# Value products in float16 halves, a score bound of 53, a branch marked ahead and the second norm by blocks, in a transformer layer

## The reference

```
q, k, v = lora(x, Wq..), lora(x, Wk..), lora(x, Wv..)     # x @ W.T + 2 * x @ B.T @ A.T
s = q k / 4 + slope[h] * (i - j);  s = -1e30 where j > i
a = softmax(s) v @ Wp.T
x1 = layernorm(x + a)
gates, experts = top-2 of softmax(x1 @ Wg), normed; rows over the capacity are dropped
y = sum over the two of gate * (gelu(x1 @ W1[e] + b1[e]) @ W2[e] + b2[e])
out = layernorm(x1 + y)
```

## Time and profile before

| | us |
|---|---|
| median of 3 runs (lowest, highest) | 1194.21 (1194.05, 1194.89) |
| the profiled execution | 1195.21 |
| its span, first to last instruction | 1193.2 |
| busy in it: TensorE, ScalarE, VectorE | 1124.1, 867.6, 629.0 |
| exponentials, first start to last end | 29.0 to 760.5 |

### The profile page before, as it was taken

One profiled execution on the slowest core, in us unless ns is written; L12 is line 12 of the kernel. 1 busy time (PEld: TensorE's weight loads), 2 busy tenths in 40 slices (PEclk: granted clock), 3 DMA queues, 4 the chain that ended last, 5 costly groups with the idle time before them and its releaser, 6 DMA issues. The chain is left out here.

```text
span 1193.2 us, 23954 instructions
## 1 busy us (share of the span) xinstructions
PE 1124.1 (94%) x8592; PEld 503.7 (42%) x8592; DVE 629.0 (53%) x1832; ACT 867.6 (73%) x1109; POOL 300.4 (25%) x377
## 2 busy tenths in 40 slices
PE   9999999999999999999999979879999999999980
PEld 4333232222323222222222111267777777777760
DVE  5744342232366435734352401558777777777757
ACT  2889999999999999999999999434334433433315
POOL 5521111111123222230323120022333333333340
PEclk9999999999999999999999999979999999999995
DMA  6843341422321331122321100263553652552217
GB/s 180 186 108 82 91 95 51 94 68 88 93 75 57 113 71 60 53 89 68 83 70 43 44 19 17 91 183 49 119 114 48 134 118 32 124 133 27 25 19 282
DMA packets 119301, 104.20 MB, mean 87 GB/s; under 512 B 59223, under 2 KB 104508, under 8 KB 119184
## 3 DMA queue, kind: packets, MB, share of 16 engines
q1 hardware_dynamic: 101720, 76.90, 24.8%
q0 software_dynamic: 15968, 24.12, 9.3%
q10 hardware_dynamic: 1496, 1.68, 0.5%
HBM read 48.07 MB, written 47.96 MB: 80 GB/s over the span
## 5 line engine op out<-in xcount | busy, mean ns | idle before, releaser
L1502 ACT ACTIVATE prob<-ps_s 128x1024 f32<-128x1024 f32 (+4 forms) x841 | 703.8, 981 | 28.9 <-PE ps_s L1382 27.0
L1401 PE MATMUL ps_o<-prob,v_aug 128*17 128x512 f32 (+3 forms) x3236 | 404.0, 567 | 8.8 <-ACT prob L1502 5.8
L2469 ACT ACTIVATE hid<-ps_h,b 128x384 f32<-128x384 f32 (+1 forms) x192 | 107.3, 560 | 229.1 <-PE ps_h L2412 223.5
L1382 PE MATMUL ps_s<-qop,kop 51*128 51x512 f16 (+3 forms) x1618 | 252.4, 368 | 10.8 <-ACT prob L1502 4.4
L1382 PEld LDWEIGHTS ps_s<-qop,kop 51*128 51x128 f16 x1618 | 61.7, 93 | 334.1 <-ACT prob L1502 307.1
L2428 PE MATMUL ps_y<-w2s,hs 128*128 128x256 bf16 (+1 forms) x1728 | 189.8, 273 | 0.1
L1586 DVE COPY acc<-ps_o 32x512 f32<-32x512 f32 (+2 forms) x108 | 74.2, 687 | 218.8 <-PE ps_o L1401 216.4
L2412 PE MATMUL ps_h<-xs,w1s 128*128 128x384 bf16 (+1 forms) x1152 | 186.4, 315 | 0.0
L2386 POOL DMA_INDIRECT result<-y,entry x72 | 116.5, 1618 | 249.0 <-DVE y L2500 218.3
L2428 PEld LDWEIGHTS ps_y<-w2s,hs 128*128 128x128 bf16 (+1 forms) x1728 | 160.0, 99 | 25.4 <-issue 3.1
L1538 POOL TENSOR_SCALAR_AFFINE_SELECT prob<-prob 128x256 f32<-128x256 f32 (+1 forms) x179 | 69.3, 400 | 300.1 <-ACT prob L1502 298.2
(11 more groups left out here) (201 smaller groups left out, 688.0 us busy)
## 6 DMA issues: line engine op xcount, KB each, us to landing
w<-in_W SPq DMA_DIRECT2D x16, 1024.0 KB, 7.9
slots_x<-empty POOLq DMA_DIRECT2D x12, 520.0 KB, 3.9
qop<-fparts_q SPq DMA_DIRECT2D x42, 128.0 KB, 4.8
aT<-attnT SPq DMA_DIRECT2D x16, 256.0 KB
x_all<-in_x SPq DMA_DIRECT2D x8, 512.0 KB
result<-x_all SPq DMA_DIRECT2D x8, 512.0 KB, 3.5
x_all<-result SPq DMA_DIRECT2D x8, 512.0 KB, 7.2
out<-x_all SPq DMA_DIRECT2D x8, 512.0 KB, 2.6
```

The source lines that it names most:

```text
L1382: mm = pe.matmul(ps_s[:, u.p % SLOTS_S, e, a.q0:], o.key(e, a.h, a.kt), o.query(e, a.h, a.b, a.q0), start=True, stop=True)
L1401: mm = pe.matmul(ps_o[32 * c:32 * c + VW, a.q0:], o.v[:, a.kt, a.h], prob[:, t % RING, c % 2, c // 2, a.q0:], start=a.first, stop=a.last)
L1502: act.activation(prob[:, t % RING, n, e:z, q0:], ps_s[:, u.p % SLOTS_S, e:z, q0:], ACT.Exp, scale=1.0 / (SCALE * SCALE)).then_inc(exp_done, 1)
L2469: act.activation(hid[:, q % HB, 0:w], ps_h[:, q % HB, 0:w], ACT.Gelu_apprx_tanh, bias=b1[:, e, q % HC:q % HC + 1]).then_inc(gelu, 1)
```

## The change

The bound falls from 55 to 53, and with it the tiles of four heads; the plan of turns and all tables are new. Values of blocks 2 to 7 are made from the float16 halves of x and of the value weights, which are split once (dve_split_values, at SPLIT_V_AT; their largest value joins the test). The general path, which used values made in float32, now makes them itself. Because value tiles read the halves of x, these can be overwritten later only; the splits move to 2 and 1 turns ahead of the first half tile and the reductions to 1 and 3 turns after it. The flag is loaded 4 turns ahead of the branch, the place is marked as the hint of the branch, and the branch is written with br_ne. The second norm goes by single blocks; ScalarE takes the root (function Sqrt, warmed by one instruction right behind the experts), VectorE its reciprocal and one Newton step.

```diff
-BOUND = 55.0
+BOUND = 53.0
...
 LATER = [int(c) for c in
-            ('6664664226425344534642334246422334264245645445534246424444444246424435345364534453453444444642424344'
...
+            ('4664564234534454534642434246423445353133444455342345323453423345323344233555555645453534446645556456'
-HALF_AT = {2: (17, 19, 21, 23, 25, 27, 29, 31), 3: (45, 47, 51, 55, 57, 59, 63, 67), 4: (87, 89, 95, 97, 100, 103, 106, 111), 5: (135, 139, 141, 148, 151, 154, 160, 164), 6: (193, 200, 205, 208, 212, 216, 225, 229), 7: (264, 266, 271, 277, 285, 294, 296, 298)}
+HALF_AT = {2: (17, 19, 21, 23, 25, 27, 29, 31), 3: (45, 47, 50, 54, 56, 58, 61, 66), 4: (87, 89, 94, 96, 98, 100, 102, 109), 5: (133, 136, 138, 146, 148, 152, 157, 161), 6: (191, 198, 203, 206, 210, 213, 222, 224), 7: (260, 263, 269, 273, 281, 291, 293, 295)}
-NORM_AT = {0: 4, 1: 15, 2: 33, 3: 69, 4: 114, 5: 168, 6: 236, 7: 305}
+NORM_AT = {0: 4, 1: 14, 2: 33, 3: 68, 4: 113, 5: 166, 6: 232, 7: 302}
-VALUE_AT = {0: (0, 2), 1: (6, 9, 11, 13), 2: (35, 37, 39, 41), 3: (71, 73, 81, 84), 4: (118, 121, 128, 132), 5: (175, 177, 180, 188), 6: (239, 243, 250, 261), 7: (309, 324, 326, 335)}
+VALUE_AT = {0: (0, 2), 1: (6, 8, 10, 12), 2: (35, 37, 39, 41), 3: (70, 73, 80, 84), 4: (116, 120, 126, 130), 5: (173, 175, 178, 186), 6: (236, 240, 247, 256), 7: (306, 319, 324, 330)}
-SETUP_TURN, BOUND_TURN = 76, 338
+SETUP_TURN, BOUND_TURN = 75, 334
...
+SPLIT_V_AT = {5: 0, 7: 1, 9: 2, 11: 3}
...
         if _p[2:] == (0, 0):
             for _k in range(4):
-                SPLIT_X_AT[_t - 5 + _k] = (_p[1], _k)
+                SPLIT_X_AT[_t + (-2, -1, 1, 3)[_k]] = (_p[1], _k)
+            assert _p[1] == 2 or VALUE_AT[_p[1] - 1][-1] < _t - 2
...
+ANNOUNCED = 4
...
+@contextmanager
+def only_if(nc, eng, name, announced):
+
+    flag, at = announced
+    eng.br_ne(flag, 0, on_true=name + "_taken", on_false=name + "_past").branch_hint(at)
+    with nc.body(name + "_taken", valid_engines=bass.OrderedEngineSet([eng.engine])):
+        yield
+        eng.br(name + "_past")
+    nc.switch_bb(name + "_past")
...
     def pe_value(j, pe, n, s, out):
-        pe.wait_ge(j.x_loaded[n % 2], 16 * (n // 2 + 1))
-        for c in range(2):
-            mm = pe.matmul(out, j.xT[:, n % 2, c, s * P:(s + 1) * P], j.weff[:, 2, c, :], start=(c == 0), stop=(c == 1))
+        cols = slice(s * P, (s + 1) * P)
+        if n < 2:
+            pe.wait_ge(j.x_loaded[n], 16)
+            for c in range(2):
+                mm = pe.matmul(out, j.xT[:, n, c, cols], j.weff[:, 2, c, :], start=(c == 0), stop=(c == 1))
+        else:
+            pe.wait_ge(j.wv_done, 3)
+            pe.wait_ge(j.xs_done, n - 1)
+            for i, (a, b) in enumerate(FPARTS):
+                for c in range(2):
+                    mm = pe.matmul(out, j.xs[:, a, c, cols], j.wv_low[c] if b else j.wv_high[:, c],
+                                   start=(i == 0 and c == 0), stop=(i == len(FPARTS) - 1 and c == 1))
         mm.then_inc(j.v_mm, 1)
...
+    def dve_split_values(j, dve, k):
+
+        w = j.weff[:, 2]
+        if k == 0:
+            dve.wait_ge(j.weff_done, 6)
+            dve.wait_ge(j.w_loaded, 16 * 2)
+            dve.tensor_scalar(j.wv_high, w, SCALE, None, ALU.mult).then_inc(j.wv_done, 1)
+        elif k == 1:
+            dve.wait_ge(j.wv_done, 1)
+            for c in range(2):
+                dve.scalar_tensor_tensor(out=j.wv_low[c], in0=w[:, c], scalar=SCALE, in1=j.wv_high[:, c], op0=ALU.mult,
+                                         op1=ALU.subtract).then_inc(j.wv_done, 1)
+        else:
+            dve.tensor_reduce(j.peak[:, k - 2, NB - 1:], j.wv_high.rearrange("p c d -> p (c d)"), AX.X,
                               (ALU.max, ALU.min)[k - 2]).then_inc(j.peaks, 1)
...
     def dve_split_x(j, dve, n, k):
...
             if n > 2:
-                dve.wait_ge(j.proj_mm, j.done(n - 1, 3))
+                dve.wait_ge(j.v_mm, n * KT)
...
     def dve_value(j, dve, n, s, bank):
         dve.wait_ge(j.v_mm, n * KT + s + 1)
-        dve.tensor_copy(j.o.v[:, n * KT + s, :, 0:DH], bank[:, 0:D].rearrange("p (h d) -> p h d", h=H)).then_inc(j.v_out, 1)
-        dve.tensor_copy(j.r.xg[:, n * KT + s], bank[:, D:D + E]).then_inc(j.v_out, 1)
+        scale = 1.0 if n < 2 else 1.0 / SCALE
+        dve.tensor_scalar(j.o.v[:, n * KT + s, :, 0:DH], bank[:, 0:D].rearrange("p (h d) -> p h d", h=H), scale, None,
+                          ALU.mult).then_inc(j.v_out, 1)
+        dve.tensor_scalar(j.r.xg[:, n * KT + s], bank[:, D:D + E], scale, None, ALU.mult).then_inc(j.v_out, 1)
...
     def flag_of(j, eng):
         eng.wait_ge(j.bnd_step, 11)
-        return eng.value_load(j.flag[0:1, 0:1], min_val=0, max_val=1)
+        flag = eng.value_load(j.flag[0:1, 0:1], min_val=0, max_val=1)
+        return flag, eng.mark_branch_hint_location()
...
+                    if t == FLAG_TURN - ANNOUNCED:
+                        announced = j.flag_of(pe)
                     if t == FLAG_TURN:
-                        y.tensor(pe, j.flag_of(pe))
+                        y.tensor(pe, announced)
...
-    GROUPS = [(0, 1), (2, 3), (4, 5), (6,), (7,)]
-    WIDEST = 2
+    TILES = NB * KT
+    GROUPS = [(n * KT, (n + 1) * KT) for n in range(NB)]
+    BY_VECTOR = KT // 2
+    FINISH = 5
...
     def sync(z, sp):
         for n in range(NB):
             sp.dma_start(z.z[:, n], z.src[n]).then_inc(z.loaded[n], 16)
         for n in range(NB):
-            sp.wait_ge(z.applied, KT * (n + 1) if n < NB - 1 else KT * n + KT // 2)
+            sp.wait_ge(z.applied, KT * (n + 1) if n < NB - 1 else KT * (n + 1) - z.BY_VECTOR)
             if n == NB - 1:
-                sp.wait_ge(z.applied_last, KT // 2)
+                sp.wait_ge(z.scales, z.FINISH * len(z.GROUPS) + z.BY_VECTOR)
             sp.dma_start(z.dst[n], z.z[:, n]).then_inc(z.stored, 16)
         sp.wait_ge(z.stored, 16 * NB)
 
-    def scalar(z, act):
-        for g, blocks in enumerate(z.GROUPS):
-            act.wait_ge(z.scales, g + 1)
-            for n in blocks:
-                for s in range(KT if g < len(z.GROUPS) - 1 else KT // 2):
-                    act.activation(z.z[:, n, s], z.z[:, n, s], ACT.Identity, scale=z.rstd[:, n, s:s + 1],
-                                   bias=z.nmr[:, n, s:s + 1]).then_inc(z.applied, 1)
+    def scalar(z, act, some):
+        act.activation(z.warm[:], some, ACT.Sqrt)
+
+        def root(g):
+            a, e = z.GROUPS[g]
+            act.wait_ge(z.spread_step, 2 * e + g + 1)
+            act.activation(z.root[:, a:e], z.v[:, a:e], ACT.Sqrt).then_inc(z.roots, 1)
+
+        root(0)
+        for g, (a, e) in enumerate(z.GROUPS):
+            if 0 < g < len(z.GROUPS) - 1:
+                root(g + 1)
+            act.wait_ge(z.scales, z.FINISH * (g + 1))
+            for i in range(a, min(e, z.TILES - z.BY_VECTOR)):
+                n, s = divmod(i, KT)
+                act.activation(z.z[:, n, s], z.z[:, n, s], ACT.Identity, scale=z.rstd[:, i:i + 1],
+                               bias=z.nmr[:, i:i + 1]).then_inc(z.applied, 1)
+                if i == a + 1 and g == 0:
+                    root(1)
 
     def vector(z, dve):
 
-        c = Chain(dve, z.step, 0, RSQRT_STEPS * len(z.GROUPS))
-        d = Chain(dve, z.spread_step, 0, 2 * KT * NB)
-        for s in z.spread(d, 0):
+        d = Chain(dve, z.spread_step, 0, 2 * z.TILES + len(z.GROUPS))
+        for _ in z.spread(d, 0):
             pass
-        for g, blocks in enumerate(z.GROUPS):
+        for g in range(len(z.GROUPS)):
             later = z.spread(d, g + 1) if g + 1 < len(z.GROUPS) else iter(())
-            n0, w = blocks[0], len(blocks)
-            mean, var = z.mv[:, n0:n0 + w, :, 0], z.mv[:, n0:n0 + w, :, 1]
-            rstd = z.rstd[:, n0:n0 + w]
-            tmp = [z.tmp[:, k, 0:w] for k in range(5)]
-            d.wait()
-            for k, _ in enumerate(rsqrt_pieces(c, var, tmp, rstd)):
-                if k >= 3:
+            next(later, None)
+            for _ in z.finish(dve, g):
+                if g:
                     next(later, None)
-            c.wait()
-            dve.scalar_tensor_tensor(out=z.nmr[:, n0:n0 + w], in0=mean, scalar=-1.0, in1=rstd, op0=ALU.mult,
-                                     op1=ALU.mult).then_inc(z.scales, 1)
-            if g == len(z.GROUPS) - 1:
-                n = blocks[0]
-                for s in range(KT // 2, KT):
-                    dve.tensor_scalar(z.z[:, n, s], z.z[:, n, s], z.mv[:, n, s, 0:1], z.rstd[:, n, s:s + 1],
-                                      ALU.subtract, ALU.mult).then_inc(z.applied_last, 1)
             for _ in later:
                 pass
-        c.end()
+        for i in range(z.TILES - z.BY_VECTOR, z.TILES):
+            n, s = divmod(i, KT)
+            dve.tensor_scalar(z.z[:, n, s], z.z[:, n, s], z.mv[:, i, 0:1], z.rstd[:, i:i + 1],
+                              ALU.subtract, ALU.mult).then_inc(z.scales, 1)
         d.end()
 
+    def finish(z, dve, g):
+
+        a, e = z.GROUPS[g]
```

(75 more changed lines are left out.)

88 lines of the change are left out of this document (46 added, 42 removed).

## The result

The changed kernel takes 1189.17 us (median; 1186.51 to 1193.89) against 1195.05 for the kernel before, run beside it: ratio 0.995, 95% interval 0.9932 to 0.9968. Faster by 6 us, not by 14, and outside the range (1175 to 1187). The profiled execution took 1189.33 us around a span of 1187.6.

A forecast was written before the change was run, and what follows sets the result against it. ScalarE's exponentials were taken to set the pace in attention, TensorE only locally. The terms -8.1 - 1.5 - 3.5 - 1.2 = -14.3 us gave a median of 1179.9 us, range 1175 to 1187.

The forecast's parts named there:

- Exponentials, -8.1: Attention: bound 53 cuts exponentials from 841 to 833, 8.1 us less on ScalarE, the pacing engine.
- Branch, -3.5: Branch to the general path: early flag load and announced jump shrink TensorE's 3.63 us gap, saving 3.5 us.
- Rival A: Branch: the announcement doesn't help and the 3.6 us gap stays, giving 1183.4 us; chance 0.10.
- Second norm, -1.2: Last stage: single blocks scale the first tile 4.3 us sooner, then VectorE sets the pitch; 1.2 us less.
- Rival C: Second norm: each of eight blocks pays two table loads on ScalarE, 20.5 us, giving 1200.4 us; chance 0.03.
- Values and new tables, -1.5: Attention, blocks 2 to 7: float16 values save TensorE 7.4 us, of which 1.5 us come back, new tables included.
- at best 5 go, at worst 6 come: Attention: range for values and new tables, from 14.9 us of ScalarE waits in two stretches.
- That cover is large.: Attention: scaled evictions add at most 0.06 us each on VectorE, busy 41% there, so it has room.
- Rival B: Attention: late splits of x stall TensorE six times, +6.6 us, giving 1186.5 us; chance 0.05.
- one to three: Attention: turns by which the splits of x now stand ahead of first use, instead of three to five.

The follow-up runs named there:

- e2: The kernel before with only the branch marked four turns ahead: 1190.66 us, ratio 0.998 to the kernel before.
- e1: The kernel before with only the second norm of the change: 1193.71 us, ratio 0.9992 to the kernel before.
- e8: The kernel after with the reductions of x's halves cut to 16 columns, the rest left out: 1189.37 us, ratio 0.9945 to the kernel before.
- e9: The kernel after with GpSimd's split also waiting until VectorE has counted the block's choices, nothing left out: 1181.98 us, ratio 0.9891 to the kernel before.
- e11: The kernel before with only GpSimd's split waiting for VectorE's counts of the choices: 1191.8 us, ratio 0.9973 to the kernel before.
- e6: The kernel after with x split earlier for blocks 3 to 5, blocks 3 and 4 in own buffers: 1186.15 us, ratio 0.9925 to the kernel before.
- e3: The kernel before with float16 values, late splits of x and the new second norm, old tables and bound: 1198.52 us, ratio 1.0045.
- e10: The kernel after with the changes of e9 and e6 together: 1179.85 us, ratio 0.9861 to the kernel before.
- e12: e9 with the values of all blocks in float32, so no half of x is split late: 1183.02 us, ratio 0.9904 to the kernel before.
- e4: The kernel after with float32 values and early splits of x, new tables, bound, branch and norm kept: 1188.89 us, ratio 0.9949.

## Why the prediction was wrong

**Exponentials, -8.1: right.** The work fell by 7.8 us.

**Branch, -3.5: right in the kernel after.** ScalarE's waits there fell by 4.1 us (5.0 to 0.9). Alone, in e2, the marking gave 2.3 us of waits and 2.4 us of time. Rival A is out: the gap of 3.6 us is gone. The Trainium skill's stall behind a branch (Runtime: NRT & Kernel Launch, "Instruction fetch mechanics") still fits the kernel before; the runs add that an announced jump shortens it, to a gap of 1.07 us in the kernel after and 2.25 in e2. How much was the flag's load, moved with the announcement, was not tried apart.

**Second norm, -1.2: right in kind, sized too small.** -2.1 in the profile; the ratio of e1 gives -1.0 and can't be told from none. The pitch was 2.2 us for the 2.3 of the sum, the root 0.20 for 0.24, and ScalarE hardly waits from block 2 on. Rival C is out: one further table load, 1.28 us at 1145.75, in idle time.

**Values and new tables, -1.5: the step that failed.** It said "I take -1.5 us for this part with the new tables [...] at best 5 go, at worst 6 come". Outside the branch the exponentials' waits rose by 10.2 us (page totals less the first wait and the branch: 22.6 before, 32.9 after). The range, like the sum, was drawn from the stretches 20 to 110 and 400 to 710 us; the largest growth, 5.7 us, is between them, from 250 to 400. It fails in three places.

1. *"That cover is large."* I priced VectorE's side by its share, 41% busy. e8 took work off it and gained nothing. What counts is what stands in its queue ahead of an eviction at the moment TensorE needs the bank. There the operations of `choose`, 0.19 us each when undisturbed, last up to 2.2 us beside GpSimd's split. That was in the profile before: `clogit` took 1.01 us in it, `gap` 0.86. I never asked why 4 columns take 0.86 us. e9 and e11 put 7 us on this in the kernel after and 3 in the kernel before, so 4 of the missing ones. A share of it is the clock: the same stop near 393 us costs ScalarE 3.05 us with the clock at 1.00 (e6) and 3.79 to 4.69 with a fall to 0.50. The sum had such a fall at the branch only.
2. *The late splits of x.* Rival B, with a chance of 0.05 and +6.6 us. Its mechanism is real: TensorE waits for half tiles 7.5 us in all with the old tables (e3, 5.4 from 110 us on); with the new ones 3.1 (1.6 from 110 us on, 1.5 ahead of it), and perhaps 3 us of the time (e6, and e10 over e9, each with overlapping intervals). The price is half of B's, since three to five of six blocks wait, not all. The splits proper stand two turns and one turn ahead of their use, where they stood five and four; the prediction's "one to three" and "three to five" blur that.
3. *The new tables' first turns.* From 20 to 110 us the waits are 11.2 to 14.5 us in the eight kernels with the new tables other than e12 (10.4), and 8.6 to 10.0 in those with the old. There is no split of GpSimd's there, and e4 (13.1) has no float16 values and no late split, so it comes with the order of turns. Part of it is a load. In all nine kernels with the new tables TensorE waits near 49 us until queries have been loaded, and in none of the five with the old. The kernel after, then e10:

```profile
49.21 0.37 PE L1443 MATMUL ps_s<-qop,kop 51*128 51x512 f16 x2 [1.74 <-DMA qop<-fparts_q]
...
50.82 0.58 PE L1446 MATMUL ps_s<-qop,kop 51*128 51x512 f16 x2 [3.75 <-DMA qop<-fparts_q]
```

This wait is 0.5 to 3.8 us long, and in five of the nine the granted clock falls behind it (0.83 on average from 50 to 60 us in the kernel after, 0.66 in e10, 1.00 before). It is likely a large part of why this stretch differs so much between kernels that are alike there. In e12, where the load costs 0.53 us and no half of x is late, the waits behind the first exponential are 8.5 us up to 110, against 7.6 in the kernel before. Another wait of the kernel after, 1.67 us at 94.40, follows 24 products in a row of three turns (2.55 us at 91.48); e12 has it too (1.98). All this is read, not tested: how much of the time the first turns cost, 1 to 4 us, stays open.

I had treated the new tables as numbers that follow from the smaller bound. They are an order of work; nothing in my sum asked what that order puts behind what.

## What to carry to other kernels

Look at the shortest operations of a busy queue: one of 4 columns that lasts five times its usual time is a sign that another engine holds something, and it costs whatever is queued behind it, not its own length, and at times a fall of TensorE's clock on top, if TensorE stops for it. Where VectorE has a chain with two SBUF inputs that somebody waits for, let GpSimd's long pass wait for the end of the chain by a semaphore: here one line gave more than the change's other parts but one. A later place in an engine's own order delays nothing when that engine is otherwise idle. And price a new schedule as a part of its own: ask what it puts behind what, and which loads it needs sooner.
